# Gated cross-attention block on one core: one load queue in order of need, and a reordered first slot

## The reference

```
q      = layernorm(x) @ W.T + b
logits = q @ ctx.T + (1 - mask) * -1e9
x      = x + tanh(g_xattn) * softmax(logits) @ ctx
x      = x + tanh(g_ffn)   * layernorm(x) @ sign(W_ffn).T
```

## Time and profile before

| | us |
|---|---|
| median of 3 runs (lowest, highest) | 298.14 (297.14, 298.19) |
| the profiled execution's own time | 297.72 |
| span of its profile | 295.9 |
| PE busy | 285.6 (97%) |
| ACT, DVE, POOL busy | 253.9, 250.6, 214.1 |

### The profile page before, as it was taken

The page is one execution under the profiler, slowest core; times in us unless marked ns, Lnnn a source line. Parts: engine busy times, 40 slices in busy tenths (PEclk is TensorE's granted clock), DMA queues, the critical chain, the costliest instruction groups (busy, mean ns, idle before and its releaser), DMA issues.

```text
span 295.9 us, 9253 instructions
## 1 busy us (share of the span) xinstructions
PE 285.6 (97%) x2338; PEld 275.4 (93%) x2338; DVE 250.6 (85%) x785; ACT 253.9 (86%) x738; POOL 214.1 (72%) x585
## 2 busy tenths in 40 slices
PE   7799999999999999999999999999999999999982
PEld 6599999999999999999999999999999999999972
DVE  3578988988898898889889888988988898898883
ACT  2689999999999998999999999999989999999841
POOL 2667777778777777877777787777778777777543
PEclk9999999999999999999999999999999999999998
DMA  6933445554544555454445545544654544441112
GB/s 192 281 90 115 149 143 154 188 167 145 161 153 142 159 184 168 137 167 154 141 156 184 171 140 160 153 143 155 184 172 138 167 151 143 154 151 71 73 56 88
DMA packets 33538, 44.39 MB, mean 150 GB/s; under 512 B 3504, under 2 KB 17136, under 8 KB 33520
## 3 DMA queue, kind: packets, MB, share of 16 engines
q1 hardware_dynamic: 32416, 43.66, 46.3%
q10 hardware_dynamic: 1104, 0.53, 0.6%
HBM read 27.40 MB, written 16.78 MB: 149 GB/s over the span
## 4 chain that ended last, share of the span: by engine, by line
PE 91%; DMA 3%; POOL 2%; DVE 1%; issue 1%; ACT 1%; SPq 1%; POOLq 0%; ACTq 0%
PE ffn_ps L673 20%; PE pv_ps L655 18%; PE l_ps L636 16%; PE ctx_ps L568 11%; PE x1t_ps L642 9%; PE xt_ps L601 9%; PE pt_ps L619 5%; PE ctx_ps L560 3%; DMA x_in<-in_x_dram 3%; POOL rstd L275 1%; POOL y L313 0%; DVE x_lo L529 0%; DVE c L518 0%; ACT ffn_scaled L402 0%; POOLq L50 0%
## 5 line engine op out<-in xcount | busy, mean ns | idle before, releaser
L275 POOL TENSOR_TENSOR rstd<-ve,minus_half 128x2 f32<-128x2 f32 x128 | 89.0, 695 | 10.0
L636 PE MATMUL l_ps<-m_sb,x_t 128*128 128x77 f32 x512 | 78.8, 257 | 0.9 <-ACT m_sb L352 0.5
L636 PEld LDWEIGHTS l_ps<-m_sb,x_t 128*128 128x128 f32 x512 | 74.6, 191 | 1.4 <-ACT x_t L378 1.3
L339 ACT ACTIVATE xs<-x_in,shift,rstd 128x256 f32<-128x256 f32 x126 | 74.6, 593 | 1.0 <-POOL shift L286 1.0
L642 PE MATMUL x1t_ps<-ident,x 128*128 128x128 f32 x256 | 68.8, 273 | 0.0
L655 PE MATMUL pv_ps<-ctx_v,p_t 77*128 77x256 f32 x256 | 66.1, 380 | 0.0
L673 PE MATMUL ffn_ps<-wf_t,x_hi 128*128 128x256 f32 x256 | 56.5, 301 | 2.5 <-DVE x_lo L529 2.4
L537 DVE SCALAR_TENSOR_TENSOR x<-pv_ps,c,x_in 128x256 f32<-128x256 f32 x128 | 55.3, 472 | 0.0
L414 ACT ACTIVATE prob<-neg_l,neg_max 128x77 f32<-128x77 f32 x128 | 44.6, 351 | 10.1 <-DVE neg_max L521 10.1
L313 POOL TENSOR_TENSOR y<-ffn_scaled,x 128x256 f32<-128x256 f32 x64 | 46.3, 724 | 9.2 <-ACT ffn_scaled L402 9.2
L529 DVE TENSOR_TENSOR x_lo<-x1t_ps,x_hi 128x512 fp32r<-128x512 f32 x64 | 43.9, 686 | 9.6 <-ACT x_hi L409 9.6
(11 more groups left out here) (49 smaller groups left out, 477.8 us busy)
## 6 DMA issues: line engine op xcount, KB each, us to landing
x_in<-in_x_dram SPq DMA_DIRECT2D x64, 256.0 KB, 2.7
out_dram<-y SPq DMA_DIRECT2D x64, 256.0 KB, 2.1
ctx_v<-in_ctx_dram SPq DMA_DIRECT2D x32, 154.0 KB
mask_in<-in_mask_BxSxS_ik_dram SPq DMA_DIRECT2D x32, 154.0 KB, 3.1
wq_raw<-in_L_xattn_W_dram ACTq DMA_DIRECT2D x1, 256.0 KB, 4.2
wf_raw<-in_L_ffn_weight_dram ACTq DMA_DIRECT2D x1, 256.0 KB, 5.6
bq_col<-in_L_xattn_b_dram ACTq DMA_DIRECT2D x1, 1.0 KB, 4.5
g_raw<-in_g_xattn_dram ACTq DMA_DIRECT2D x1, 0.5 KB, 6.2
```

Source lines behind the costliest of these rows:

```text
L275: pool.tensor_tensor(res[:, i], ve[:, i], minus_half[:], ALU.pow).then_inc(res_done, 1)
L339: act.activation(xs[:, n % 2, j], x_in[:, n % N, j], ACT.Identity, scale=rstd1[:, n % R, j:j + 1], bias=shift1[:, n % R, j:j + 1]).then_in ...
L636: ins = pe.matmul(l_ps[:, j * K:(j + 1) * K], x_t[:, r % 2, c, j * P:(j + 1) * P], m_sb[:, c, r % R], start=(c == 0), stop=(c == C - 1))
```

## The change

Loads: the two weight loads move from ACT's queue to SP's, `W` behind the first x, `W_ffn` behind the second pair's context. ACT keeps the bias and the gates. POOL computes the negated mask of row 1 in the prologue. ACT in slot 0 does the exponentials of row 0, `x_t` of row 1 and the tanh first, then the keys, `m_sb`, and both halves of row 2. DVE takes the moments of row 2 after the logits of row 0. PE does 4 warm-ups in slot 0 in place of 8, and the transposes of row 1 ahead of the second pair's keys.

```diff
@@ sync
             load_x(0, 0)
+            sp.dma_start(wq_raw[:], w_q.rearrange("(c p) i -> p c i", c=C)).then_inc(wq_loaded, DMA)
             load_ctx(0, 0)
             load_x(0, 1)
             load_mask(0, 0)
             load_x(0, 2)
             load_ctx(0, 2)
+            sp.dma_start(wf_raw[:], w_ffn.rearrange("(c p) i -> p c i", c=C)).then_inc(wf_loaded, DMA)
             load_x(0, 3)
@@ gpsimd
             negmask(0)
+            negmask(1)
             norm1(2)
...
-                if exists(t0, r + 1):
+                begins = isinstance(t, int) and t == 0
+                if exists(t0, r + 1) and not begins:
                     pool.wait_ge(mask_loaded[(r + 1) % N // 2], landed(t0, r + 1))
                     at_least(pool, logits_done, t)
...
-                if exists(t0, r + 1):
+                if exists(t0, r + 1) and not begins:
                     negmask(r + 1)
@@ scalar
-            act.dma_start(wq_raw[:], w_q.rearrange("(c p) i -> p c i", c=C)).then_inc(wq_loaded, DMA)
...
-            act.dma_start(wf_raw[:], w_ffn.rearrange("(c p) i -> p c i", c=C)).then_inc(wf_loaded, DMA)
...
+                begins = isinstance(t, int) and t == 0
+                if begins:
+                    exponentials(t0, r)        # the old L410 to L417, as a function
+                    transposed_x(t0, r + 1)
+                    gates()
                 if r % 2 == 0 and exists(t0, r + 2):
                     keys_step(2 * t + 5)
...
-                if exists(t0, r + 2):
+                if exists(t0, r + 2) and not begins:
                     scale_rows(t0, r + 2, 0)
...
-                if exists(t0, r + 1):
+                if exists(t0, r + 1) and not begins:
                     transposed_x(t0, r + 1)
+                if exists(t0, r + 2) and begins:
+                    scale_rows(t0, r + 2, 0)
                 if exists(t0, r + 2):
                     scale_rows(t0, r + 2, 1)
@@ vector
             stats1(1)
-            stats1(2)
...
                 if isinstance(t, int) and t == 0:
+                    stats1(2)
                     stats1(3)
@@ tensor
                 if begins:
-                    warm_up(8)
+                    warm_up(4)
+                    transpose_x(t0, r + 1)
                     pair_keys(t0, r)
...
-                if exists(t0, r + 1):
+                if exists(t0, r + 1) and not begins:
                     transpose_x(t0, r + 1)
```

More of the change, by code:

```diff
@@ L388, in gates, with exponentials @@
                 act.activation(g_tanh[:], g_raw[:], ACT.Tanh).then_inc(tanh_ready, 1)
+            def exponentials(t0, r):
+                act.wait_ge(logits_done, t0 + r + 1)
+                at_least(act, pt_psum, t0 + r - 1)
+                for j in range(T):
+                    ins = act.activation(prob[:, r % 2, j], neg_l[:, r % 2, j], ACT.Exp, scale=-1.0,
+                                         bias=neg_max[:, r % R, j:j + 1],
+                                         accum_out=prob_sum[:, r % R, j:j + 1])
+                ins.then_inc(exp_done, 1)
             def slot(t0, r):
@@ L409, in slot @@
                     act.activation(x1_hi[:, r % 2], x1t_ps[:], ACT.Copy).then_inc(hi_done, 1)
[L410 to L419, removed]
+                if exists(t0, r) and not begins:
+                    exponentials(t0, r)
                 if r % 2 == 0 and exists(t0, r + 2):
```

## The result

| | before | after |
|---|---|---|
| median (lowest, highest), 15 runs of each | 297.79 (297.14, 472.82) | 300.27 (297.40, 302.42) |
| the profiled execution's own time | 297.72 | 299.85 |
| span of its profile | 295.9 | 298.1 |
| PE busy | 285.6 | 285.7 |

The change makes the kernel slower: the ratio of times is 1.0063, with a 95% interval of 1.0043 to 1.0084. (It is worked out from undisturbed runs alone, so the 472.82 and two runs of after over 302 us don't enter, and it is not the quotient of the medians.) The forecast was no measurable change, 298.1, with a range up to 299.3; the median lies above it. PE's work is the same; 2.2 us were added to the span.

What follows compares the result with a forecast made beforehand. PE-bound; the chain of DVE and ACT from x row 4's landing was taken to fix PE's position at 18.67 us. Terms of 0.0 left 297.72 at 297.7, given as 298.1 for the median; range 297.0 to 299.3.

Steps and rivals of the forecast that it cites:

- Bias and gates first on ACT: Start loads: 4-byte elements make the first context 0.5 us later, row 0's logits 0.25, hidden by DVE and PE idle time.
- Rival 2: Start: bias and gates delay the first context by 1.7 us, everything follows; total +0.95, 299.1; chance 0.15.
- Rival 3: PE's clock falls to 1.2 GHz at gaps of about 1.0 and 0.5 us after 11.95; 299.7; chance 0.03.
- Loads on one queue: SP's queue: only the loads' order changes, x row 4 lands no earlier; term 0.0.
- Exponentials and rows 1 first: Slot 0: exponentials 2.2 us earlier, product with context 0.4, nothing passed on past x row 4's chain; term 0.0 us.
- Masks early: POOL's prologue: row 1's mask done earlier, but DVE was not waiting for it; term 0.0.

Runs made afterwards that it cites:

- e4: After with 28 warm-ups in place of 16 ahead of the first keys; 298.68, ratio 1.0032 to before.
- e1: Before with only the two weight loads moved to SP's queue; 299.71 against 297.45, ratio 1.0078.
- e14: e13 (bias left out) with only W moved, to second on SP's queue; 301.29, ratio 1.0128 to before.
- e17: After with the gates' loads issued behind ACT's first copy of keys, tanh moved to slot 1, 22 warm-ups; 297.73 against before's 297.67, ratio 1.0005.
- e3: After without the bias load, gates issued only once the first context has landed; 301.02, ratio 1.0080 to before.
- e13: Control: e2's order without the bias load; ACT's queue holds W, FFN weight, gates; 298.10, ratio 1.0013 to before.
- e7: Before with 8 warm-ups in place of 16, so PE idles ahead of an undelayed context; 298.06, ratio 1.0030.
- e10: After with W back on ACT's queue ahead of the bias, FFN weight still on SP's; 298.59, ratio 1.0031 to before.
- e2: After with all loads as in before, so only the new order of work remains; 297.60, ratio 1.0003 to before.
- e11: e2 with only DVE's signs of the FFN weight moved ahead of row 0's logits; 297.90, ratio 1.0007 to before.
- e8: e2 with DVE's signs ahead of row 0's logits and ACT's row 2 scaling behind the copy of row 0's probabilities; 296.85 against before's 297.56, 0.9974.
- e5: After without the bias load, gates on SP's queue behind x row 2, 28 warm-ups; 299.82, ratio 1.0075 to before.
- e15: e14 (bias left out) with the gates ahead of the FFN weight on ACT's queue; 302.45, ratio 1.0157 to before.
- e9: After without the bias load, gates issued behind ACT's first copy of the keys, 22 warm-ups; 301.49, ratio 1.0116 to before.
- e12: Before with only DVE's signs of the FFN weight worked out early, its loads and slot order kept; 299.47, ratio 1.0052.

## Why the prediction was wrong

**The failed step is "Bias and gates first on ACT".** It gave the first context 0.5 us of delay, hid that behind idle time of DVE and PE, and put PE's clock at nothing. In the profiled executions the context was 1.7 us late (after), 1.4 (e4) and 0.7 (e1), and row 0's logits 2.6, 1.1 and 2.4. Three things were wrong in it.

First, the length of the gates' loads. The share was read rightly: the earlier trace rows gives the large loads' queue 46% beside small packets, and in after it has 43.0% over the 2.4 us of the gates. But the step took the bias's rate, 42 packets in 0.2 us, for the gates, and so 1.2 us for 256 elements; 274 packets took 2.4 us in after and 285 took 3.8 us in e14. At its worst, from 5.8 to 6.2 us of after, q1 had 5.9%.

Second, it treated the small loads as a cost that is paid once wherever it stands, and charged only the bias. In before the gates were last on ACT's queue behind two weights of 256 KB, and their packets ran from about 7 us on, after the first context had landed. Taking the weights away moved the gates, which the diff doesn't touch, about 3 us towards the front. Holding them back again takes the loss away with the weights where they are (e17).

Third, `W` ahead of the context on the same queue stands in no term for the context. It costs 0.3 to 0.5 us without any small load (e3 against e13 and before). e17 shows that this much is hidden when PE is kept busy, as the step had said of its 0.5.

Two readings under the step were wrong as well. The 6 warm-ups between keys and `m_step` took 1.09 us in before, not 0.8 at 130 ns each, and the keys ahead of them 0.78, where the next pair's took 0.43: there PE was still coming up from the lower level, so there was no spare 0.25 us. And four loads of x, not five, stand ahead of row 4; that entered no sum.

**Rival 2 named a good part of the mechanism** ("slower by the small loads", 0.15), with 1.7 us of delay and 299.1. That after's profile shows the same 1.7 is luck: the rival's was the middle of two bounds, and e4 and e1 have 1.4 and 0.7. Its handing-on was right: DVE does rows 2 and 3 behind the late logits and everything follows. The product with the context was 2.17 late, not 0.95, because the clock came on top.

**Rival 3, the clock, had 0.03** and is about half of the loss. The prediction looked for its trigger in the gaps behind 12 us, where the durations stayed short. It was the wait for the context: PE idles 2.03 us between two groups of warm-ups, and its work from 7.24 to about 10.3 us runs at the lower level. In before the same wait was 0.3. e4 takes this share away (1.0063 to 1.0032), e7 produces it alone (1.0030). The two rivals weren't independent: a late load is an idle PE, and they should have been priced together.

**"Loads on one queue: 0.0"** held for x row 4 in after, since DVE came later than the load, but not by itself: with the FFN weight on SP's queue, and the gates earlier for it, row 4 is 0.4 us late (e10), and the time about 0.28% longer. The queues' bytes were the same; the moment at which SP's loads got their turn was not.

**"Exponentials and rows 1 first: 0.0"** was right almost row by row once the loads were put back (e2): `m_step` of the second pair 12.95 forecast, 13.01 measured; row 1's logits 13.85 and 13.86; product 15.4 and 15.44; row 4's moments 12.87 and 12.85; row 1's masked logits 16.72 and 16.84; probabilities 18.0 and 18.11. Row 0's logits themselves were 0.28 late in e2 (9.72). Also right is what was said to bound PE there, the chain of row 4, signs and row 1's logits; but it wasn't alone. e11 takes the signs out of it and gains nothing, e8 needs ACT's order as well. **Masks early** cost nothing in e2.

**Left open.** Why the gates' loads slow transfers in the other queue too. How the delay splits: `W`'s place (0.3 to 0.5 us, e3) and the gates are told apart only by single profiled executions, and the same order of loads gave keys at 6.20, 6.94 and 7.24. The bias's own share seems small: with it, and the gates late, the context lands at 6.19 (e17), without it at 6.02 (e3, by the chain of waits). And e17 differs from after in three points at once. Warm-ups alone bring 1.0063 to 1.0032 (e4, with 28 of them); that the rest, down to 1.0005, is the gates' doing rests on e4 against e17, whose intervals barely overlap, and on the low DMA rates wherever the gates' packets run (after, e5, e13, e14, e15). After with 22 warm-ups and nothing else changed was not run.

## What to carry to other kernels

Before a load is moved off a queue, list what stood behind it there and what will run in its place: here the new order of loads gained nothing and cost 0.6% (0.8% in e1). Here the loads of many single 4-byte elements did no harm once they stood behind the first tiles, with their consumer moved as well (e17; without that move, e9, they cost more than before). And while the first tiles land keep PE fed up to the moment they arrive; then read each delay at the start twice, once as time and once as clock.

## What the hardware showed that was not expected

- While two loads that give one 4-byte element to 128 partitions each ran, the whole DMA traffic was low: 382 GB/s in the microsecond before, 79 GB/s over the next 3 us (e14); 2 GB/s over one microsecond when they were on the same queue as the large loads (e5). The drop isn't always so deep: in before, with the gates in flight from 7 to 9 us, it is 202 and 219 GB/s. The bias, 256 single elements, does it too, for a shorter time: from 3 to 4 us e17 moves 96 GB/s, and e9, the same loads without the bias, 316.
- After 2.03 us of idling PE ran its next 3 us of work at the lower level (after; e7 did the same after 1.86 us, and e1 after 1.00 us for 5 us, while after 0.87 and 0.74 us, in e3 and e13, the next warm-ups took 0.82 us, the higher level). The granted clock of these stretches reads 1.00; only the durations show it.
- The granted clock fell to 0.50 for some 4 us in e12 and in e9 (behind 3.11 us of idling; busy 0.57 of 2 us from 14 to 16). Of after's 15 executions 5 had a mean under 0.993 and were 2 us slower; the others still spread over more than 3 us, so this is not the whole of its scatter.
